# One-head attention pass of a graph network: node-block steps at fixed phases of a slot

## The chip, the cores and the metric

The kernel runs on one core of one Trainium2 chip. The metric is the device time of one execution in microseconds (us). Lower is better.

## What is computed

A graph of 3125 nodes (128 features each) and 103125 edges sorted by destination goes through four residual layers. The third is a pair of GATv2 layers, the fourth a pair of typed transformer layers. Cut to what matters here:

```python
def gatv2(x, src, dst, Wl, bl, Wr, br, att, bias, heads, out_ch):
    xl = (x @ Wl + bl).reshape(n, heads, out_ch)
    xr = (x @ Wr + br).reshape(n, heads, out_ch)
    e = leaky_relu(xl[src] + xr[dst], 0.2)
    score = einsum('ehc,hc->eh', e, att)
    smax = segment_max(score, dst)
    ex = exp(score - smax[dst])
    alpha = ex / (segment_sum(ex, dst)[dst] + 1e-16)
    return segment_sum(xl[src] * alpha, dst) + bias      # plus self loops
...
x = x + gatv2(relu(gatv2(layernorm_relu(x), ..., heads=4)), ..., heads=1)
h = layernorm_relu(x)
k, q, v = (typed_linear(h, node_type, W) for W in (Wk, Wq, Wv))   # 8 node types
kw, m = rel_apply(k, edge_type, Watt), rel_apply(v, edge_type, Wmsg)  # 8 relations
```

The typed layer's key and value are made for all eight relations of a node at once, before its edges are looked at, and are gathered by edge afterwards.

## The kernel before, in words

The nodes lie in 25 blocks of 128 (numbered k, in the order in which their edges are processed). The edges are cut into 830 tiles of 128, none across two blocks, and 16 tiles make a group; there are 52 groups. Six passes go over all groups: one weighted sum, then attention passes 1 to 5. This case is about pass 3, the GAT with one head (H = 1), from about 3325 to 4491 us of the span. Its node-block work is class `AfterGats`: when all edges of a block have been summed, the block's attention is finished, its features are normalized, and the typed key, query and value tables that pass 4 reads are made and written.

In `attention_pass` (L924) each engine runs its own list of slots. Slot s does the first half of group s (gathered rows plus destination rows, leaky relu, scores) and the second half of group r = s - 1 (segment maxima by scans, exponentials, weighted rows, sums). All queues are in order and wait on semaphores.

- POOL (`gather_rows`, L749 to L763) issues 16 indirect DMAs a group (L761), into one of 4 buffers. It waits until group s - 4 has been weighed.
- PE in slot s (L1347 to L1392): destination rows of products 0 (L1293), `turn_scores(r)` (L1308, L1310), own rows 0 (L1302), destination rows 1, hooks 0 and 1, `spread_drop` (L1317), `turn_back` (L1322, L1324), hook 2, destination rows 2, hook 3, sums 0 to 2 (L1341, a unit of up to three tiles each), own rows 2, hook 4, destination rows 3, sums 3, hook 5, sums 4 and 5, hook 6, hook 7.
- DVE in slot s (L1212 to L1271): the rest of the additions of group s - 2 (L1201) around the scans of tiles (L1128, L1129), hooks 0 and 1, the chain over tiles with product 0 in it (L1140 to L1176), score 0 (L1122), `rescale` (L1182), hook 2, last maxima and weighing (L1186, L1189), hook 3, product and score 1 (L1111, L1113, L1122), additions 0, hook 4, additions 1 and 2, hook 5, product and score 2, additions 3, hook 6, product and score 3, hook 7.
- ACT in slot s (L1069 to L1088): `keep_scores` (L1045), hook 0, `keep_column` (L1027), hook 1, `open_scale` (L1049, an exponential), `exps` (L1053), `exp_columns` (L1058), `weigh_tiles` (L1066), hooks 2 to 6, `keep_linear` (L1038), hook 7.
- SP issues the loads of one-hot matrices and flags of the next slot, with hooks 0 to 3 ahead of the flags and 4 to 7 behind them.

A hook is a place where the node-block work stands in an engine's list. Hook number x counts 8 a slot, so x = 8s + h. `first(k)` (L1469) gives the x at which block k begins, and each step of the block has an offset d from it: step d runs at x = first(k) + d. With `last_tile(k)` in group s at place t, `first` is 8(s + 1) + 6 where t < 11 and 8(s + 2) otherwise. So the phase (the hook within a slot) of every step differs between the two kinds of blocks. Blocks 9 to 13, 23 and 24 are of the second kind, the other eighteen of the first. A block is 33.2 tiles, so a new one begins nearly always two slots after the one before (three once, from 13 to 14).

The node-block steps of `AfterGats` (L2163 to L2259), before:

- DVE: d = 0 own shares (L1918 to L1929), d = 3 the new features and their statistics (L1938 to L1941, L2220 to L2222, L1513 to L1515), d = 6 `standard` (L1526, L1527), d = 9 `by_type` (L2094: the turned block times eight type masks).
- ACT: d = 2 exponential (L2235), d = 5 square root (L1520), d = 7 normalized features (L2240) and clearing of the sums (L2242), d = 13 `take_kv`, `take_query` (L2136, L2141), d = 15, 17, 19, 21 `take_relations` 0 to 3 (L2151).
- PE: d = 8 `turn` (L2085), d = 11 `key_and_value` (L2106, 16 products), d = 12 `query` (L2113), d = 14, 16, 18, 20 `relations` 0 to 3 (L2129). `relations` i waits until ACT has taken i - 1 (L2126).
- SP: d = -4 load of the block's masks (L2069), d = 26 write of the block's table (L2160).

An ACT table load stands in ACT's list just ahead of the first instruction that needs another table: one of L1520 (square root) and one of L1049 (exponential) for each block.

Of the kernel before, what the change touches and what calls it, by code (L numbers as in the profile page):

```python
# [14 lines left out]
P = 128  # L15
# [9 lines left out]
J = 4  # L25
GT = GC * J
NT_MAX = (E + NB * (P - 1)) // P
NG = (NT_MAX + GT - 1) // GT
# [15 lines left out]
TYPES = 8  # L44
# [7 lines left out]
HOOKS = 8  # L52
# [26 lines left out]
class Chain:  # L79


    def __init__(self, sem):
        self.sem, self.n = sem, 0
# [1349 lines left out]
def last_tile(k):  # L1433

    return (k + 1) * NT_MAX // NB - 1
# [19 lines left out]
class After:  # L1455


    LAST = 0
    EARLY = 0

# [8 lines left out]
    def first(self, k):  # L1469

        s, t = divmod(last_tile(k), GT)
        return HOOKS * (s + 1) + 6 if t < ON_TIME else HOOKS * (s + 2)

    def due(self, x):

        return [(k, x - self.first(k)) for k in range(NB) if -self.EARLY <= x - self.first(k) <= self.LAST]

    @property
    def end(self):
        return self.first(NB - 1) + self.LAST + 1  # L1480

# [9 lines left out]
    def load(self, sp, s):  # L1491
        pass

    def sp(self, sp, x):
        pass

    def act(self, act, x):
        pass

    def pe(self, pe, x):  # L1500
        pass

    def dve(self, dve, x):
        pass
# [25 lines left out]
class AfterL0(After):  # L1530


    LAST = 13

# [236 lines left out]
class AfterL1(Projected):  # L1771


    LAST = 23

# [132 lines left out]
def own_shares(after, dve, c, k, H, att):  # L1908

    e, V = after.e, after.nc.vector  # L1910
    hs = D // H
    W = hs + 1
    a = e.acc[:, k * AW:k * AW + H * W].rearrange("p (h c) -> p h c", c=W)
    edge_max = e.acc[:, k * AW + H * W:k * AW + H * W + H]
    own, em, top = after.scalars(k, 0, H), after.scalars(k, 4, H), after.scalars(k, 8, H)
    share = after.scalars(k, 32, 2 * H)
    t = after.t
    c.step(dve, V.tensor_tensor(t, e.xlN[:, k, :], e.kN[:, k, :], ALU.add))  # L1918
    if H == 1:
        c.step(dve, V.scalar_tensor_tensor(t, t, 0.0, att, ALU.max, ALU.mult, accum_out=own))  # L1920
    else:
        c.step(dve, V.scalar_tensor_tensor(t, t, 0.0, att, ALU.max, ALU.mult))
        c.step(dve, V.tensor_reduce(own, t.rearrange("p (h c) -> p h c", h=H), AX, ALU.add))
    c.step(dve, V.tensor_tensor(own, own, e.xlW[:, k, D:D + H], ALU.add))
    c.step(dve, V.tensor_scalar(em, a[:, :, hs], 0.5, -BIG, ALU.is_lt, ALU.mult))
    c.step(dve, V.tensor_tensor(em, em, edge_max, ALU.add))
    c.step(dve, V.tensor_tensor(top, em, own, ALU.max))
    V.tensor_tensor(share[:, 0:H], em, top, ALU.subtract)
    return V.tensor_tensor(share[:, H:2 * H], own, top, ALU.subtract)  # L1929


def scaled_shares(after, dve, c, k, H):

    e, V = after.e, after.nc.vector
    W = D // H + 1
    a = e.acc[:, k * AW:k * AW + H * W].rearrange("p (h c) -> p h c", c=W)
    den, share = after.scalars(k, 12, H), after.scalars(k, 32, 2 * H)
    c.step(dve, V.tensor_tensor(den, a[:, :, W - 1], share[:, 0:H], ALU.mult))  # L1938
    c.step(dve, V.tensor_tensor(den, den, share[:, H:2 * H], ALU.add))
    c.step(dve, V.reciprocal(den, den))  # L1940
    return V.tensor_tensor(share.rearrange("p (n h) -> p n h", n=2), share.rearrange("p (n h) -> p n h", n=2),  # L1941
                           den.unsqueeze(1).to_broadcast([P, 2, H]), ALU.mult)


class AfterGat(Projected):


    LAST = 16

# [76 lines left out]
BANDS = 4  # L2026
# [4 lines left out]
class Typed(After):  # L2031


    def __init__(self, nc, A, e, name):
        super().__init__(nc, A, e, name)
        ar = e.arena
        self.kqv, self.bd = ar[:, 0:3072], ar[:, 3072:3584]
        self.stage, self.kvS = ar[:, 3584:5632], ar[:, 5632:5888]
        self.temps = [ar[:, 5888 + P * n:5888 + P * (n + 1)] for n in range(5)]
        self.mask, self.hTm = ar[:, 6528:7040].bitcast(BF16), ar[:, 7040:8064]  # L2040
        self.wa = ar[:, 8064:9088]
        self.left, self.right = e.ps[:, 7, 0:256], e.ps[:, 7, 256:512]
        self.corner = e.ps[:, 7, 384:512]
        self.pri = e.small[:, 320:320 + RELS]

    def load_typed(self, sp, n, name, layer, home, done):
# [32 lines left out]
    def turn(self, pe, src, ready, k, free, frees):  # L2079

        S, nc = self.S, self.nc
        pe.wait_ge(S[ready], k + 1)
        if frees > 0:
            pe.wait_ge(S[free], frees)
        nc.tensor.transpose(self.corner, src, self.e.ident[:, :]).then_inc(S["turned"], 1)  # L2085

    def by_type(self, dve, n, k, free, frees):

        S, V = self.S, self.nc.vector
        dve.wait_ge(S["mask_here"], 16 * (k + 1))  # L2090
        dve.wait_ge(S["turned"], n)
        if frees > 0:
            dve.wait_ge(S[free], frees)
        V.tensor_tensor(self.hTm.rearrange("p (t n) -> p t n", t=TYPES), self.corner.unsqueeze(1).to_broadcast([P, TYPES, P]),  # L2094
                        self.mask.rearrange("p (t n) -> p t n", t=TYPES), ALU.mult).then_inc(S["masked"], 1)

    def key_and_value(self, pe, k, masked):
# [65 lines left out]
class AfterGats(Typed):  # L2163


    LAST = 26
    EARLY = 4

    def __init__(self, nc, A, e):
        super().__init__(nc, A, e, "n4")  # L2170
        self.t = self.temps[0]
        self.att, self.b2 = e.vecs[:, D:2 * D], e.vecs[:, 256:384]

    def load(self, sp, s):

# [14 lines left out]
    def sp(self, sp, x):  # L2190

        for k, d in self.due(x):
            if d == -4:
                self.load_mask(sp, k, 1)
            elif d == 26:
                self.write(sp, k, self.e.t3_d[0])

    def close(self, sp):
# [3 lines left out]
    def dve(self, dve, x):  # L2202

        e, S, nc, V = self.e, self.S, self.nc, self.nc.vector
        c = self.chain
        if x == 0:
            V.memset(self.bd, 0.0).then_inc(S["bd_zero"], 1)
        if x == 44:
            self.scale_relations(dve, c)
        for k, d in self.due(x):  # L2210
            xk = e.xN[:, k, :]
            if d == 0:
                self.summed(dve, k)
                own_shares(self, dve, c, k, 1, self.att).then_inc(S["shares"], 1)
            elif d == 3:
                dve.wait_ge(S["exp_made"], k + 1)
                if k == 0:
                    dve.wait_ge(S["v"], 16)
                c.step(dve, scaled_shares(self, dve, c, k, 1))
                c.step(dve, V.scalar_tensor_tensor(self.t, e.acc[:, k * AW:k * AW + D], self.scalars(k, 32, 1), self.b2, ALU.mult, ALU.add))  # L2220
                c.step(dve, V.scalar_tensor_tensor(self.t, e.xlN[:, k, :], self.scalars(k, 33, 1), self.t, ALU.mult, ALU.add))
                c.step(dve, V.tensor_tensor(xk, xk, self.t, ALU.add))  # L2222
                self.statistics(dve, c, k, xk, "var")
            elif d == 6:
                self.standard(dve, c, k, "std").then_inc(S["scale"], 1)
            elif d == 9:
                self.by_type(dve, k + 1, k, "q_done", k)

    def act(self, act, x):

        e, S, nc = self.e, self.S, self.nc
        for k, d in self.due(x):
            if d == 2:
                act.wait_ge(S["shares"], k + 1)
                nc.scalar.activation(self.scalars(k, 32, 2), self.scalars(k, 32, 2), ACT.Exp).then_inc(S["exp_made"], 1)  # L2235
            elif d == 5:
                self.deviation(act, k, "var", "std")
            elif d == 7:
                act.wait_ge(S["scale"], k + 1)
                nc.scalar.activation(e.hN[:, k, :], e.xN[:, k, :], ACT.Relu, bias=self.scalars(k, 27, 1), scale=self.scalars(k, 29, 1))\  # L2240
                    .then_inc(S["h_made"], 1)
                nc.scalar.activation(e.acc[:, k * AW:(k + 1) * AW], e.acc[:, k * AW:(k + 1) * AW], ACT.Copy, scale=0.0)  # L2242
            elif d == 13:
                self.take_kv(act, k)
                self.take_query(act, k)
            elif d in (15, 17, 19, 21):
                self.take_relations(act, k, (d - 15) // 2)

    def pe(self, pe, x):

        for k, d in self.due(x):
            if d == 8:
                self.turn(pe, self.e.hN[:, k, :], "h_made", k, "rel_taken", BANDS * k)
            elif d == 11:
                self.key_and_value(pe, k, k + 1)
            elif d == 12:
                self.query(pe)
            elif d in (14, 16, 18, 20):
                self.relations(pe, k, (d - 14) // 2)  # L2259


class FromLayer(Typed):
# [87 lines left out]
class AfterTyped(FromLayer):  # L2350


    LAST = 25
    EARLY = 1

# [67 lines left out]
class AfterAll(FromLayer):  # L2423


    LAST = 20
    EARLY = 1

# [102 lines left out]
```

## Time and profile before

| | |
|---|---|
| median of 3 runs | 6829.93 us (6827.04 to 6832.83) |
| profiled execution | 6820.63 us, span 6818.9 us |
| busy share of the span | PE 69%, PE weight load 58%, DVE 73%, ACT 24%, POOL 70% |
| mean granted TensorE clock | 0.767 |

Times in the rows below are us from the start of the span. A line of the timeline gives the start, the busy time, engine, line of the kernel, operation and operands, how many instructions run together (xN), and in brackets the idle time of the engine just before with what ended it. A line of a stretch gives its two ends, its length, the busy time and number of instructions of each engine (of PE, PE weight load, DVE, ACT and POOL where all are shown, of the one engine where one line of the kernel is), the granted TensorE clock as a share of full speed, the DMA share and GB/s.

### The profile page before, as it was taken

How to read it: one execution, taken by the hardware profiler on the slowest of the kernel's cores; microseconds unless marked ns; L12 is line 12 of the kernel's file. 1: busy time of each engine (PE TensorE's matmuls, PEld its weight loads, DVE VectorE, ACT ScalarE, POOL GpSimd, SP SyncE). 2: the span in 40 equal slices, each digit the busy share in tenths (PEclk: the TensorE clock that was granted, in tenths of full speed). 3: DMA queues.
4: the chain of work that ended last, by engine and by line, in shares of the span. 5: the costliest groups of instructions: out<-in, count | busy, mean ns of one | idle time of the engine just before them, and what ended most of it. 6: DMA issues, size and time to landing. Idle time of an engine off the chain costs nothing. (4 is left out here: it accounts for less than half of the span.)

```text
span 6818.9 us, 92826 instructions
## 1 busy us (share of the span) xinstructions
PE 4690.2 (69%) x26423; PEld 3981.3 (58%) x26423; DVE 4946.8 (73%) x14307; ACT 1667.5 (24%) x5320; POOL 4761.5 (70%) x4997
## 2 busy tenths in 40 slices
PE   3555555666666678787688888857777776676665
PEld 2444444555555566666566666646776765565665
DVE  5434433888888688888688778857777775888887
ACT  3333332122222111111133323312222221112121
POOL 5777776777776677777577777547666663777775
PEclk8676676777776788888789889967778776777777
DMA  5444445666665455545455555556666664666665
GB/s 163 167 160 161 160 153 159 214 212 218 208 217 179 143 165 161 169 157 166 131 189 185 171 177 183 168 175 224 215 226 223 213 214 135 219 218 228 217 230 157
DMA packets 407533, 1266.66 MB, mean 186 GB/s; under 512 B 128582, under 2 KB 189766, under 8 KB 320630
## 3 DMA queue, kind: packets, MB, share of 16 engines
q1 hardware_dynamic: 200000, 760.73, 30.6%
q0 software_dynamic: 199760, 495.12, 26.2%
q10 hardware_dynamic: 7270, 4.88, 0.3%
q8 instruction: 221, 3.62, 0.2%
q14 instruction: 282, 2.31, 0.1%
HBM read 1083.37 MB, written 176.98 MB: 185 GB/s over the span
## 5 line engine op out<-in xcount | busy, mean ns | idle before, releaser
L761 POOL DMA_INDIRECT gathered_rows<-table_l,arena x3048 | 2915.2, 956 | 1073.7 <-issue 911.9
L1201 DVE TENSOR_TENSOR acc<-acc,ps 128x136 f32 (+2 forms) x4160 | 1209.0, 291 | 520.3 <-PE ps L1341 360.3
L1293 PEld LDWEIGHTS ps<-dst_side,onehot_t 128*128 128x128 f32 x8320 | 1312.0, 236 | 445.5 <-issue 369.8
L1293 PE MATMUL ps<-dst_side,onehot_t 128*128 x8320 | 1421.0, 326 | 184.9 <-issue 106.4
L761 POOL DMA_INDIRECT gathered_rows<-table_l,src_rel_edges x1116 | 1060.6, 950 | 624.5 <-issue 329.3
L1341 PE MATMUL ps<-weighted_rows,onehot 128*128 128x136 f32 (+2 forms) x8320 | 1281.3, 315 | 13.7 <-DVE acc L1201 10.1
L1341 PEld LDWEIGHTS ps<-weighted_rows,onehot 128*128 128x128 f32 x8320 | 1226.7, 227 | 46.1 <-issue 35.1
L1122 DVE TENSOR_REDUCE scores<-products 128x16 f32<-128x512 f32 (+2 forms) x1040 | 711.4, 684 | 27.1
L907 PE MATMUL ps<-gathered_rows,onehot 128*128 128x128 f32 x1664 | 340.6, 369 | 471.1 <-ACT gathered_rows L833 469.7
L761 POOL DMA_INDIRECT arena<-table_l,src_rel_edges x544 | 516.2, 949 | 189.1 <-issue 161.8
L863 DVE TENSOR_TENSOR acc<-acc,ps 128x128 f32 x832 | 238.4, 286 | 532.9 <-PE ps L907 500.3
L907 PEld LDWEIGHTS ps<-gathered_rows,onehot 128*128 128x128 f32 x1664 | 294.9, 266 | 525.8 <-ACT gathered_rows L833 525.5
L1317 PE MATMUL ps<-open_node_drop,ones 64*128 64x4 f32 (+2 forms) x520 | 129.4, 319 | 511.0 <-DVE open_node_drop L1158 511.0
L1189 DVE TENSOR_TENSOR weighted_rows<-gathered_rows,ps 128x512 f32<-128x512 f32 x732 | 454.2, 679 | 5.6 <-ACT weighted_rows L1058 5.0
L1317 PEld LDWEIGHTS ps<-open_node_drop,ones 64*128 64x128 f32 (+2 forms) x520 | 108.9, 260 | 571.7 <-DVE open_node_drop L1158 569.2
L1302 PE MATMUL ps<-gathered_rows,ident 128*128 128x512 f32 x624 | 398.5, 725 | 32.8 <-DMA gathered_rows<-table_l,arena 32.7
L1117 DVE TENSOR_TENSOR products<-gathered_rows,ps 128x512 f32<-128x512 f32 x420 | 284.8, 678 | 139.4 <-DMA gathered_rows<-table_l,src_rel_edges 71.0
L833 ACT ACTIVATE gathered_rows<-gathered_rows,arena 128x128 f32<-128x128 f32 x832 | 264.9, 391 | 436.3 <-DMA gathered_rows<-table_l,arena 436.2
L761 POOL DMA_INDIRECT arena<-table_l,arena x272 | 258.6, 951 | 82.9 <-issue 81.3
L2129 PE MATMUL ps<-arena 32*128 32x256 f32 x800 | 268.2, 461 | 33.0 <-ACT arena L2151 31.3
L1322 PE MATMUL ps<-ident,exp_scores_t 64*128 64x64 f32 (+2 forms) x260 | 99.5, 383 | 275.9 <-ACT exp_scores_t L1053 275.9
L1115 DVE SCALAR_TENSOR_TENSOR products<-ps,vectors 128x512 f32<-128x512 f32 x312 | 210.9, 676 | 101.0 <-PE ps L1302 99.9
(321 smaller groups left out, 6206.5 us busy)
## 6 DMA issues: line engine op xcount, KB each, us to landing
onehot_t<-onehots_turned SPq DMA_DIRECT2D x260, 1024.0 KB, 5.3
onehot<-onehots SPq DMA_DIRECT2D x260, 1024.0 KB
onehots<-onehot SPq DMA_DIRECT2D x52, 1024.0 KB, 6.8
onehots_turned<-onehot_t SPq DMA_DIRECT2D x52, 1024.0 KB, 4.3
table_l<-arena SPq DMA_DIRECT2D x50, 1024.0 KB
gathered_rows<-table_l,arena POOLq DMA_INDIRECT x3048, 2.5
segment_flags_sb<-segment_flags SPq DMA_DIRECT2D x1300, 8.2 KB
arena<-type_mask_rows SPq DMA_DIRECT2D x75, 256.0 KB
```

Source lines behind the costliest of these rows:

```text
L761: pool.indirect_dma_start(out=home(v, t // GC)[:, t % GC, :], out_offset=None, in_=table, in_offset=bass.IndirectOffsetOnAxis(ap=index[:, ...
L833: ins = nc.scalar.activation(weighed[:, u, t, :], rv[:, u, t, :], ACT.Copy, scale=e.ewE[:, bass.ds(s * GT + t, 1)])
L863: V.tensor_tensor(a, a, ps[:, bank(u, j), g * P:g * P + D], ALU.add).then_inc(e.added.sem, 1)
L907: ins = nc.tensor.matmul(ps[:, bank(u, j), g * P:g * P + D], e.oh[:, u, GC * j + g, :], weighed[:, u, GC * j + g, :], start=True, stop=True)
L1117: ins = V.tensor_tensor(out, home(v, j)[:, :, 0:D], z, ALU.mult)
L1122: V.tensor_reduce(scE[:, GC * j:GC * (j + 1), :], e.prod[:, j % 2, :].rearrange("p (g h d) -> p g h d", g=GC, h=H), AX, ALU.add).then_inc( ...
L1189: V.tensor_tensor(exvH[:, GC * j:GC * (j + 1), :, 0:hs], home(v, j)[:, :, vrow:vrow + D].rearrange("p g (h d) -> p g h d", h=H), bc(exE[:, ...
L1201: V.tensor_tensor(a, a, ps[:, BP + n % 3, at:at + PW], ALU.add).then_inc(e.acc_step.sem, 1)
L1293: ins = nc.tensor.matmul(ps[:, BZ + k, g * P:(g + 1) * P], e.ohT[:, u, t * P:(t + 1) * P], kRows[:, bass.ds(bs[t % 8], D)], start=not by_p ...
L1302: nc.tensor.matmul(ps[:, BZ + j % 2, :].rearrange("p (g d) -> p g d", d=D), e.ident[:, :], home(v, j)[:, :, 0:D], start=False, stop=True). ...
L1341: ins = nc.tensor.matmul(ps[:, BP + n % 3, at:at + PW], e.oh[:, u, t, :], exvT[:, t, :], start=True, stop=True)
L2129: ins = mm(home, self.kvS[lane, m * P:(m + 1) * P], self.bd[lane, m * RELS * BAND:(m + 1) * RELS * BAND], start=True, stop=True)
```

## The change

`AfterGats` gets a `first` of its own: 8(s + 2) for every block. So a block always begins at hook 0 of a slot, here called its slot A, and slot B is the one behind it. With a new block every two slots, each slot A also holds the steps d = 16 to 23 of the block before, and each slot B its steps 24 to 31. All steps get new offsets. The turned block goes to bank 3 of PSUM, where the exponentials lie (columns 256 to 383), not to a corner of bank 7. So `turn` no longer waits for `rel_taken` of the block before; it waits for `masked` of the block before and, in PE's list, for the weighing by DVE of the last group. `key_and_value` now waits for `rel_taken`. In other classes the turned block stays where it was.

```diff
--- before.py
+++ after.py
@@ -2041,6 +2041,7 @@
         self.wa = ar[:, 8064:9088]
         self.left, self.right = e.ps[:, 7, 0:256], e.ps[:, 7, 256:512]
         self.corner = e.ps[:, 7, 384:512]
+        self.face = self.corner
         self.pri = e.small[:, 320:320 + RELS]
 
     def load_typed(self, sp, n, name, layer, home, done):
@@ -2082,7 +2083,7 @@
         pe.wait_ge(S[ready], k + 1)
         if frees > 0:
             pe.wait_ge(S[free], frees)
-        nc.tensor.transpose(self.corner, src, self.e.ident[:, :]).then_inc(S["turned"], 1)
+        nc.tensor.transpose(self.face, src, self.e.ident[:, :]).then_inc(S["turned"], 1)
 
     def by_type(self, dve, n, k, free, frees):
 
@@ -2091,7 +2092,7 @@
         dve.wait_ge(S["turned"], n)
         if frees > 0:
             dve.wait_ge(S[free], frees)
-        V.tensor_tensor(self.hTm.rearrange("p (t n) -> p t n", t=TYPES), self.corner.unsqueeze(1).to_broadcast([P, TYPES, P]),
+        V.tensor_tensor(self.hTm.rearrange("p (t n) -> p t n", t=TYPES), self.face.unsqueeze(1).to_broadcast([P, TYPES, P]),
                         self.mask.rearrange("p (t n) -> p t n", t=TYPES), ALU.mult).then_inc(S["masked"], 1)
 
     def key_and_value(self, pe, k, masked):
@@ -2163,13 +2164,19 @@
 class AfterGats(Typed):
 
 
-    LAST = 26
-    EARLY = 4
+    LAST = 35
+    TAKES = (24, 25, 29, 31)
+    RELATIONS = (24, 25, 28, 30)
 
     def __init__(self, nc, A, e):
         super().__init__(nc, A, e, "n4")
         self.t = self.temps[0]
+        self.face = e.ps[:, 3, 256:384]
         self.att, self.b2 = e.vecs[:, D:2 * D], e.vecs[:, 256:384]
+
+    def first(self, k):
+
+        return HOOKS * (last_tile(k) // GT + 2)
 
     def load(self, sp, s):
 
@@ -2190,9 +2197,9 @@
     def sp(self, sp, x):
 
         for k, d in self.due(x):
-            if d == -4:
+            if d == 1:
                 self.load_mask(sp, k, 1)
-            elif d == 26:
+            elif d == 35:
                 self.write(sp, k, self.e.t3_d[0])
 
     def close(self, sp):
@@ -2209,10 +2216,10 @@
             self.scale_relations(dve, c)
         for k, d in self.due(x):
             xk = e.xN[:, k, :]
-            if d == 0:
+            if d == 2:
                 self.summed(dve, k)
                 own_shares(self, dve, c, k, 1, self.att).then_inc(S["shares"], 1)
-            elif d == 3:
+            elif d == 5:
                 dve.wait_ge(S["exp_made"], k + 1)
                 if k == 0:
                     dve.wait_ge(S["v"], 16)
@@ -2221,42 +2228,45 @@
                 c.step(dve, V.scalar_tensor_tensor(self.t, e.xlN[:, k, :], self.scalars(k, 33, 1), self.t, ALU.mult, ALU.add))
                 c.step(dve, V.tensor_tensor(xk, xk, self.t, ALU.add))
                 self.statistics(dve, c, k, xk, "var")
-            elif d == 6:
+            elif d == 8:
                 self.standard(dve, c, k, "std").then_inc(S["scale"], 1)
-            elif d == 9:
+            elif d == 15:
                 self.by_type(dve, k + 1, k, "q_done", k)
 
     def act(self, act, x):
 
         e, S, nc = self.e, self.S, self.nc
         for k, d in self.due(x):
-            if d == 2:
+            if d == 3:
                 act.wait_ge(S["shares"], k + 1)
                 nc.scalar.activation(self.scalars(k, 32, 2), self.scalars(k, 32, 2), ACT.Exp).then_inc(S["exp_made"], 1)
-            elif d == 5:
+            elif d == 6:
                 self.deviation(act, k, "var", "std")
-            elif d == 7:
+            elif d == 9:
                 act.wait_ge(S["scale"], k + 1)
                 nc.scalar.activation(e.hN[:, k, :], e.xN[:, k, :], ACT.Relu, bias=self.scalars(k, 27, 1), scale=self.scalars(k, 29, 1))\
                     .then_inc(S["h_made"], 1)
                 nc.scalar.activation(e.acc[:, k * AW:(k + 1) * AW], e.acc[:, k * AW:(k + 1) * AW], ACT.Copy, scale=0.0)
-            elif d == 13:
+            elif d == 21:
                 self.take_kv(act, k)
                 self.take_query(act, k)
-            elif d in (15, 17, 19, 21):
-                self.take_relations(act, k, (d - 15) // 2)
+            elif d in self.TAKES:
+                self.take_relations(act, k, self.TAKES.index(d))
 
     def pe(self, pe, x):
 
         for k, d in self.due(x):
-            if d == 8:
-                self.turn(pe, self.e.hN[:, k, :], "h_made", k, "rel_taken", BANDS * k)
-            elif d == 11:
+            if d == 13:
+                self.e.exv_ready.wait(pe, self.a_no, J * min(x // HOOKS, NG))
+                self.turn(pe, self.e.hN[:, k, :], "h_made", k, "masked", k)
+            elif d == 16:
+                if k >= 1:
+                    pe.wait_ge(self.S["rel_taken"], BANDS * k)
                 self.key_and_value(pe, k, k + 1)
-            elif d == 12:
+            elif d == 20:
                 self.query(pe)
-            elif d in (14, 16, 18, 20):
-                self.relations(pe, k, (d - 14) // 2)
+            elif d in self.RELATIONS:
+                self.relations(pe, k, self.RELATIONS.index(d))
 
 
 class FromLayer(Typed):
```

## Rows read from the trace of the kernel before

**Rows 1.** Stretches of pass 3, DVE line L1128 alone: one scan a slot.

```profile
3805.20:4046.20 241.00, 4.12 (x10) 0.81 0.53 167
4067.30:4437.10 369.80, 7.62 (x18) 0.91 0.57 174
```

**Rows 2.** The gathers of pass 3: ns min/median/max, first and last start.

```profile
L761 POOL DMA_INDIRECT gathered_rows<-table_l,arena x830: 938/944/1384, 3324.8 to 4379.4; - x166
```

**Rows 3.** Timeline of a slot of block 11, PE and DVE.

```profile
3912.62 5.74 PE L2106 MATMUL ps<-arena 128*128 128x128 f32 x32
...
3919.07 2.71 DVE L1201 TENSOR_TENSOR acc<-acc,ps 128x130 f32 x8 [5.27 <-PE ps L1341]
```

**Rows 4.** Timeline of slots 36 and 37, DVE.

```profile
4106.16 0.69 DVE L1122 TENSOR_REDUCE scores<-products 128x4 f32<-128x512 f32 x1
...
4114.44 0.19 DVE L1186 TENSOR_TENSOR weighted_rows<-ps,arena 128x16 f32<-128x16 f32 x1 [0.39 <-ACT weighted_rows L1058]
...
4126.56 0.69 DVE L1122 TENSOR_REDUCE scores<-products 128x4 f32<-128x512 f32 x1
...
4129.56 0.10 DVE L1938 TENSOR_TENSOR row_scalars<-acc,row_scalars 128x1 f32<-128x1 f32 x1
...
4131.94 0.15 DVE L1515 TENSOR_SCALAR row_scalars<-row_scalars 128x1 f32<-128x1 f32 x1
...
4135.99 0.19 DVE L1186 TENSOR_TENSOR weighted_rows<-ps,arena 128x16 f32<-128x16 f32 x1
...
4140.75 0.94 DVE L1201 TENSOR_TENSOR acc<-acc,ps 128x130 f32 x3 [1.34 <-PE ps L1341]
...
4147.32 0.69 DVE L1122 TENSOR_REDUCE scores<-products 128x4 f32<-128x512 f32 x1
```

**Rows 5.** Timeline of slots 36 and 37, ACT.

```profile
4130.96 0.66 ACT L2151 ACTIVATE arena<-ps 128x256 f32<-128x256 f32 x2 [2.55 <-PE ps L2129]
...
4138.99 1.28 ACT L1520 ACT_TABLE_LOAD   x1
4140.28 0.20 ACT L1520 ACTIVATE row_scalars<-row_scalars 128x1 f32<-128x1 f32 x1
4141.99 0.50 ACT L2240 ACTIVATE h_nodes<-x_nodes,row_scalars 128x128 f32<-128x128 f32 x1 [1.50 <-DVE row_scalars L1527]
4142.39 0.30 ACT L2242 ACTIVATE acc<-acc 128x136 f32<-128x136 f32 x1
...
4149.09 1.28 ACT L1049 ACT_TABLE_LOAD   x1
4154.54 0.26 ACT L1049 ACTIVATE open_node_scale<-ps,open_node_column 128x1 f32<-128x1 f32 x1 [4.17 <-PE ps L1317]
```

**Rows 6.** Timeline of slots 36 and 37, PE.

```profile
4127.31 0.39 PE L1308 MATMUL ps<-ident,scores 128*16 128x128 f32 x2 [1.52 <-DVE scores L1122]
...
4129.79 1.13 PE L2129 MATMUL ps<-arena 32*128 32x256 f32 x4
4133.69 0.38 PE L1317 MATMUL ps<-open_node_drop,ones 32*128 32x1 f32 x2 [2.77 <-DVE open_node_drop L1158]
...
4137.34 2.08 PE L1293 MATMUL ps<-dst_side,onehot_t 128*128 x8
...
4149.56 1.05 PE L1293 MATMUL ps<-dst_side,onehot_t 128*128 x8
```

**Rows 7.** Stretches of slots 36 and 37: the granted clock.

```profile
4118.00:4135.20 17.20, 11.77 (x70) 8.53 (x68) 15.15 (x54) 3.15 (x12) 12.93 (x15) 1.00 0.55 175
4135.40:4142.00 6.60, 6.60 (x27) 5.76 (x28) 4.83 (x13) 4.68 (x14) 4.76 (x5) 0.50 0.22 53
```

**Rows 8.** Timeline of the pass's end: last score, last block, next pass.

```profile
4435.05 0.69 DVE L1122 TENSOR_REDUCE scores<-products 128x4 f32<-128x512 f32 x1
...
4467.12 6.71 PE L2106 MATMUL ps<-arena 128*128 128x128 f32 x32 [1.37 <-DVE arena L2094]
...
4491.26 0.06 DVE L1273 MEMSET tile_ends_turned<- 128x2 f32 x1 [24.19 <-PEq L1419]
```

## The prediction

> **What bounds the kernel now.** I read the stretches first. Only pass 3 is touched, so the question is what sets its pace. The scan of tiles runs once a slot. In one stretch it takes 369.8 us for 18 slots, 20.5 us each; in the stretch of blocks 9 to 13 it takes 241 us for 10 slots, 24.1 us each [rows 1]. Then the gathers: 830 of them start between 3324.8 and 4379.4 us, 1.27 us apart, 20.3 us a group [rows 2]. The last score of the pass ends at 4435.7 [rows 8], 56 us after the last gather was issued. So the gathers are ahead, and slots, not gathers, set the end: their pace is a floor only.
>
> The timelines say what a slot consists of. In the stretch of blocks 9 to 13 the key and value products stand at hook 3, ahead of sums 0: PE works 5.74 us on them and DVE waits 5.27 us for the sums [rows 3]. That is the cost of that phase. Two blocks' worth: a pair of slots is 48.2 us there (241/5), against 41.2 us in slots 36 and 37, from score end to score end 4106.85, 4127.25, 4148.01, that is 20.4 + 20.8 [rows 4]. Five pairs times 7 us is 35 us lost to the second phase: the most that an equal phase for all could give back, and a little of the lag if the pace came down to the floor.
>
> **The change part by part.** Nothing is added or taken from the work, apart from waits. So I take the pair 36/37 and move its steps, and then look for what is late.
>
> *Slot A* is slot 36 with these moves. Own shares go from hook 6 to hook 2, ahead of the weighing: same length, and they cover the wait of 0.39 us for the exponentials [rows 4]. The new features and statistics (from 4129.56 to 4132.09, 2.5 us [rows 4]) come in at hook 5. The products stay in the head of the slot (hook 0 for hook 1, nothing stands between). The query goes behind the sums, where PE has room. 20.4 + 2.5 - 0.4 = 22.5 us. What is late next: PE. Product 2 starts 2.5 us later, while PE has nothing else to do; by my count PE has idle times of about 1 and 2.6 us just before the head of slot B, with one destination-row batch of 1.05 us between them. The square root waits for the statistics at hook 6; `keep_linear` behind it has until the scores are made, some 4 us later, so nothing waits.
>
> *Slot B* is slot 37 without the 2.5 us of statistics, and without the 1.34 us in which DVE waits for sums [rows 4]: relation 3 of the block before no longer stands between the turning back and the destination rows (it did, until 4137.34 [rows 6]). 20.8 - 2.5 - 1.3 = 17.0 us. `standard` stays in that slot, `by_type` at hook 7 as before.
>
> Without any new wait the pair is 39.5 us. But the head of slot B now carries a queue on ACT. Behind `keep_scores` stand relation 0 taken (hook 0), `keep_column`, then at hook 1 relation 1 taken, the normalized features, the clearing, then the table load for the exponential, because the square root ran last; only then `open_scale` and `exps`, for which DVE and the whole second half of the slot wait. From the last score's end: PE has relation 0 done after 3.7 us (4127.25 to 4130.92 [rows 4, 6]); ACT takes it in 0.66; PE makes relation 1 in 1.13, which waits for that take; ACT takes it in 0.66; features and clearing are 0.8, the load 1.28, `open_scale` 0.26 [rows 5]. With small gaps that is 8.5 us, and DVE starts its last maxima some 0.9 us after it (exponentials, turning back, copy), at 9.4. In slot 37 that came at 8.7 (4135.99 [rows 4]), and 2.5 us of it were the statistics, which go, and 0.3 us is `standard`, which comes: 6.5. So slot B waits 2.9 us anew, and the pair is 42.4 us. Before, the table load ran at 4149.09, and ACT was then idle for 4.17 us, so it cost nothing [rows 5]; it loses that cover.
>
> One rule of the Trainium skill makes this worse: the page "ScalarE: Activation LUTs", section "What ACT_TABLE_LOAD costs", has a drain of about 1.38 us behind each load of 1.28. By it slot B would wait 1.4 us longer, some 30 us over the pass. Here the square root starts at 4140.28, right behind its load of 1.28 us begun at 4138.99 [rows 5]: no drain shows, so the row is used.
>
> *The clock.* After PE's idle time of 2.77 us in the head of slot 37 [rows 6] the granted clock is 0.50 for the 6.6 us that follow, after 1.00 before it [rows 7]: 1.2 instead of 2.4 GHz. A batch of destination rows takes 2.08 us in that stretch and 1.05 outside it [rows 6]. Now the idle time comes just before the head of slot B (1 and 2.6 us), so the head itself would run at the lower level, and it is the head that ACT's queue hangs on. All of the 3.7 us up to relation 0 at half speed would cost 3.6 us more, none 0. I take 2.3, nearer to the whole, since the stretch at the lower level lasted 6.6 us, but it may begin a little after the head does. A second drop behind the longer wait for ACT (about 3 us of idle PE) lies where slot 37 has its own; DVE has 3 us of its own work before it needs sums there. I take 0.5 us for it, between 0 and 3. The pair is then 45.2 us.
>
> *Smaller things.* The mask load moves from d = -4 to d = 1. On SP it stands behind `by_type` of the block before, ahead of the flags, which are due a slot later; its data have 14 hooks. The write at d = 35 has five hooks until the stage is filled again, as before. `turn` in bank 3 waits for a weighing for which sums 3 just ahead of it has already waited: nothing. POOL waits more often, being ahead: nothing.
>
> *The end of the pass.* From the last score to the next pass it is 55.5 us now, of which 24.1 follow the start of the last block's products at 4467.12 [rows 8]. The last block's own shares come some 2 us earlier. But the products, query and relations of block 23, formerly partly inside slots 51 and 52, now run after slot 52, and in ACT's list the square root and the features of block 24 stand behind takes of block 23. I count 29.6 us at full clock and 38 at half until the last products, against 31.4 now: between -2 and +7, I take +4 us.
>
> **The sum.** Seventeen pairs of the first kind (all eighteen but block 0's, which has no relations before it and stays about equal): 17 x (45.2 - 41.2) = +68. Five pairs of the second kind: 5 x (45.2 - 48.2) = -15. End: +4. Together +57 us with 45.2; I shade the pair to 44.9, as the two clock terms hardly come whole in every pair: 17 x 3.7 - 5 x 3.3 + 4 = +50 us. On the profiled execution's 6820.6 us that is 6871. The median of the runs is 9.3 us above that execution, so 6880 us.
>
> **Rivals.**
> 1. *Faster: ACT's queue doesn't bind.* If relations and takes in the head go through beside DVE's work, the pair falls to 39.5 us, under the gathers' floor of 40.6, which then sets the pace: 17 x (-0.6) + 5 x (-7.6) + 4 = -44 us, 6786. For it: ACT is busy only 24% and its wait at 4154.54 is 4.17 us of spare time [rows 5]. Against: the list is in order, and the sum of rows gives 8.5 us where 5.6 are free. It decides at 5.6 us from the last score to `open_scale`.
> 2. *The queue binds, the clock holds.* Pair 42.4: 17 x 1.2 - 5 x 5.8 + 4 = -5 us, 6825. For it: after 1.52 us of idle PE at 4127.31 [rows 6] the clock was still 1.00 [rows 7]. Against: the idle time is longer now.
> 3. *The clock stays low through all of slot B.* Then the pair is as in the second kind, 48.2: 17 x 7 + 4 = +123 us, 6953. For it: PE's busy share of a pair falls with its length. Against: that kind also had the products ahead of the sums.
>
> **How the numbers follow.** The forecast (44.9 us a pair, or anything from 43 to 47) has 0.53, rival 1 0.22, rival 2 0.17, rival 3 0.08. 0.2%, about what a measurement of this kernel can tell, is 13.7 us. Rival 2 straddles it: I give 0.12 of it to no change and 0.05 to faster. The forecast at its lowest, 43, is +9 us (17 x 1.8 - 5 x 5.2 + 4), so 0.03 of it is no change too. Faster 0.27, same 0.15, slower 0.58. The range goes from 6800, which takes in rival 2 with its spread and stops short of rival 1 whole, to 6930, the forecast at 47 us a pair (+97).
>
> **What would show it.** In the changed profile: the scan of tiles at 22 to 23 us a slot over the whole pass, with no stretch at 24.1 and none at 20.5; in slots B `open_scale` 8 to 12 us after the last score, with the table load right ahead of it and DVE idle at `rescale` by 2 to 5 us, released by ACT; the wait of 5.27 us for sums gone; the granted clock at 0.5 in the head of slots B; gathers waiting for the weighing in most slots. The prediction is wrong if `rescale` in slots B waits less than 1 us, or if the pace comes out at 20.3 us a slot. Passes other than the third should stay within a microsecond or two.

## The result, and the profile after

The changed kernel takes 6878.56 us (median of 4 runs, 6871.19 to 6884.97), the kernel before 6828.49: a ratio of 1.0077, 95% interval 1.0064 to 1.009, so 50 us slower. Forecast were 6880 us. All of it lies in pass 3. In the profiled executions it goes from first gather to next pass's first from 1167.1 to 1228.5 us, +61 us; the last score of the pass comes at 4488.1 instead of 4435.7 [rows 8], and the rest is the end and a start that differs by 5 us. The profiled execution itself took 6876.83 us, 56 more than that of before.

The stretches of the changed kernel, DVE line L1128 alone (one scan a slot; columns as in [rows 1]), from the scan of group 8 to that of group 50, and parts of it. The three parts hold 12, 10 and 14 slots; in the last two the scans at both ends are counted:

```profile
3522.00:4467.80 945.80, 17.18 (x42) 0.83 0.53 170
...
3522.10:3802.00 279.90, 4.90 (x12) 0.81 0.53 175
3847.40:4066.60 219.20, 4.10 (x11) 0.85 0.53 174
4152.60:4467.90 315.30, 5.72 (x15) 0.84 0.52 165
```

There are 42 slots in 945.8 us, 22.5 each or 45.0 us a pair; the three parts have 23.3, 21.9 and 22.5 us a slot, so none is at 20.5 and none at 24.1. The same 42 slots took 895.3 us before, at a clock of 0.88:

```profile
3518.40:4413.70 895.30, 17.75 (x42) 0.88 0.58 181
```

What DVE waited for in pass 3, changed kernel (us in total, times, longest):

```profile
DVE acc L1182 <- ACT open_node_scale L1049: 105.2, 46, 5.5
DVE acc L1201 <- PE ps L1341: 46.5, 80, 1.5
DVE tile_ends_turned L1273 <- PEq L1419: 25.9, 1, 25.9
DVE products L1115 <- PE ps L1302: 25.7, 14, 11.5
DVE weighted_rows L1186 <- ACT weighted_rows L1058: 13.2, 23, 0.6
```

and the same view of the kernel before:

```profile
DVE acc L1201 <- PE ps L1341: 65.4, 55, 5.3
DVE tile_ends_turned L1273 <- PEq L1419: 24.2, 1, 24.2
DVE products L1115 <- PE ps L1302: 21.7, 7, 12.1
...
DVE acc L1182 <- issue: 8.5, 35, 0.8
...
DVE acc L1182 <- ACT open_node_scale L1049: 4.9, 17, 0.6
```

The wait of 5.27 us for sums [rows 3] is gone: the longest is now 1.5 us. In its place `rescale` (L1182) waits 105 us for ACT, where it waited 4.9 before: 88.7 us of it in slots B, 16.1 in slots A. How, the head of one slot B shows (timelines of ACT, then PE, then DVE, changed kernel; lines behind 2041 are one higher or more than before):

```profile
4173.71 0.27 ACT L1045 ACTIVATE scores_t<-ps 16x128 f32<-16x128 f32 x1 [4.53 <-PE ps L1310]
4178.52 0.66 ACT L2152 ACTIVATE arena<-ps 128x256 f32<-128x256 f32 x2 [4.55 <-PE ps L2130]
4179.07 0.20 ACT L1027 ACTIVATE open_node_column<-onehot_t 128x1 f32<-128x1 f32 x1
4181.34 0.66 ACT L2152 ACTIVATE arena<-ps 128x256 f32<-128x256 f32 x2 [2.07 <-PE ps L2130]
4181.89 0.49 ACT L2247 ACTIVATE h_nodes<-x_nodes,row_scalars 128x128 f32<-128x128 f32 x1
4182.27 0.31 ACT L2249 ACTIVATE acc<-acc 128x136 f32<-128x136 f32 x1
4182.59 1.28 ACT L1049 ACT_TABLE_LOAD   x1
4183.88 0.26 ACT L1049 ACTIVATE open_node_scale<-ps,open_node_column 128x1 f32<-128x1 f32 x1
```

```profile
4173.06 0.39 PE L1308 MATMUL ps<-ident,scores 128*16 128x128 f32 x2 [2.40 <-DVE scores L1122]
...
4174.57 1.86 PE L1293 MATMUL ps<-dst_side,onehot_t 128*128 x8
4176.36 2.07 PE L2130 MATMUL ps<-arena 32*128 32x256 f32 x4
...
4184.39 0.28 PE L1322 MATMUL ps<-ident,exp_scores_t 16*128 16x16 f32 x1 [3.08 <-ACT exp_scores_t L1053]
```

```profile
4172.32 0.69 DVE L1122 TENSOR_REDUCE scores<-products 128x4 f32<-128x512 f32 x1
...
4184.18 0.30 DVE L1182 TENSOR_TENSOR acc<-acc,open_node_scale 128x129 f32 x1 [4.97 <-ACT open_node_scale L1049]
```

The last score ends at 4173.01, `open_scale` at 4184.14: 11.1 us later, in the order forecast, take, column, take, features, clearing, load. DVE is idle for 4.97 us. PE was idle 2.40 us ahead of the head, then its clock fell within it: the destination rows take 1.86 us and relation 0 2.07 us, not 1.13 [rows 6].

Not every slot B is like this one. In another, the clock held (PE, ACT and DVE, and the stretch, all engines, of the changed kernel):

```profile
4311.15 0.39 PE L1308 MATMUL ps<-ident,scores 128*16 128x128 f32 x2 [1.45 <-DVE scores L1122]
...
4319.27 0.26 ACT L1049 ACTIVATE open_node_scale<-ps,open_node_column 128x1 f32<-128x1 f32 x1
...
4319.56 0.30 DVE L1182 TENSOR_TENSOR acc<-acc,open_node_scale 128x129 f32 x1 [2.54 <-ACT open_node_scale L1049]
```

```profile
4311.10:4317.10 6.00, 4.74 (x24) 2.99 (x24) 5.53 (x21) 1.38 (x6) 4.48 (x6) 1.00 0.73 263
```

Here `open_scale` ends 8.4 us behind the last score (4311.09), and DVE waits 2.54 us. Of the 21 slots B with relations in their head (the last slot left out), five are so: PE was idle 1.2 to 1.6 us ahead of the head, and the granted clock of the six microseconds behind the score is 1.00. In the other sixteen PE was idle 2.40 us there, that clock is 0.55 to 0.72, `open_scale` ends 10.1 to 11.4 us behind the score, and DVE waits 3.8 to 5.5 us.

### The profile page after: what moved, and what is told of

It reads as the page before. It is cut to its first block and busy times, and to the rows that moved or that the text cites. A ratio compares the mean times of both kernels' runs of the same rounds, so it can differ in the third digit from the quotient of the medians.

```text
span 6875.1 us, 92851 instructions
## 1 busy us (share of the span) xinstructions
PE 4757.0 (69%) x26423; PEld 4031.3 (59%) x26423; DVE 4947.1 (72%) x14307; ACT 1666.6 (24%) x5320; POOL 4760.8 (69%) x4997
## 5 line engine op out<-in xcount | busy, mean ns | idle before, releaser
L1341 PE MATMUL ps<-weighted_rows,onehot 128*128 128x136 f32 (+2 forms) x8320 | 1313.1, 320 | 20.4 <-issue 12.5
L1341 PEld LDWEIGHTS ps<-weighted_rows,onehot 128*128 128x128 f32 x8320 | 1254.3, 231 | 56.2 <-issue 46.5
```

The lines of the kernel that those rows point to most:

```text
L1341: ins = nc.tensor.matmul(ps[:, BP + n % 3, at:at + PW], e.oh[:, u, t, :], exvT[:, t, :], start=True, stop=True)
```

## The experiments

Ten kernels ran. "Slot B" and offsets are as in the section on the change. The runs of before beside them had medians of 6826 to 6828 us. Runs 1 to 4 were made together on one chip. The changed kernel was not among them: its first four runs (6878.56 us) are of another time, and on that same chip it took 6894.35 us later (run 9). So a difference of some 15 us between runs 1 to 4 and the changed kernel can't be told. The scan pace is given for the 42 slots between the scans of groups 8 and 50.

**1. Relations behind.**

```diff
-    TAKES = (24, 25, 29, 31)
-    RELATIONS = (24, 25, 28, 30)
+    TAKES = (28, 29, 30, 31)
+    RELATIONS = (28, 29, 30, 31)
```

> The changed kernel with the four relation products and their takes moved out of the head of slot B, to hooks 4, 5, 6 and 7 (d = 28 to 31 on PE and ACT). ACT's queue as the cause: only features, clearing and the table load stand ahead of open_scale, which comes at about 5 us from the last score instead of 10.9; the wait of rescale in slots B falls from about 5 us to under 1, a pair from 45 us to 41, the whole by 80 to 95 us, to 6785 to 6800 us, below the kernel before. The low clock in the head as the main cause: the head is as slow as now, the wait falls by 1 us at most, 6855 us. Product 2 coming late in slot A as the cause: no change, 6878 us.

Measured: 6893.61 us (6887.91 to 6898.87), ratio 1.0097 (1.008 to 1.0114): 15 us above the first runs of the changed kernel and level with those on the same chip, so no gain, where 80 to 95 us were expected of the queue theory. The wait at `rescale` in slots B did fall to 0.2 us, as the queue theory said (38.1 us in the pass are left, nearly all in slots A), but a new one of 81.4 us stands at the scan of tiles (DVE's waits, this kernel):

```profile
DVE tile_scans L1128 <- ACT scores_t L1045: 81.4, 50, 3.7
DVE acc L1201 <- PE ps L1341: 43.9, 67, 2.8
DVE acc L1182 <- ACT open_node_scale L1049: 38.1, 24, 2.3
```

and its PE timeline says why:

```profile
4192.38 1.12 PE L2130 MATMUL ps<-arena 32*128 32x256 f32 x4
4194.25 1.12 PE L2130 MATMUL ps<-arena 32*128 32x256 f32 x4 [0.75 <-ACT arena L2152]
4195.40 2.05 PE L1293 MATMUL ps<-dst_side,onehot_t 128*128 x8
4197.38 0.61 PE L1308 MATMUL ps<-ident,scores 128*16 128x128 f32 x2
```

The score that L1308 turns was there at 4193.04, but relations 2 and 3, with the take between them, and the destination rows at the lower clock stood ahead of it in PE's list until 4197.4. I had emptied the head of slot B and filled its end. The end costs as much: from last score to last score slot B takes 18.7 us instead of 23.0, but slot A, whose scan waits for that end, 26.6 instead of 22.4. The queue moved, and the wait moved with it. So this run confirms what waits, but my sum for it was wrong, as it looked at one end of the slot only.

**2. Features behind, and 3. root behind** take parts of ACT's queue out of the head without touching the relations.

```diff
-            elif d == 9:
+            elif d == 10:
                 act.wait_ge(S["scale"], k + 1)
```

> The changed kernel with only the normalized features and the clearing moved behind the exponentials on ACT (d = 9 to d = 10, hook 1 to hook 2 of slot B): 0.8 us less ahead of open_scale. ACT's queue as the cause: 0.8 us a slot B, 18 us in all, 6861 us, with the wait of rescale about 4.2 us. Any other cause: no change, 6878 us.

```diff
-            elif d == 6:
+            elif d == 11:
                 self.deviation(act, k, "var", "std")
...
-            elif d == 9:
+            elif d == 13:
                 act.wait_ge(S["scale"], k + 1)
```

(and on DVE `standard` at 12, on PE `turn` at 14.)

> The changed kernel with the square root moved from slot A to slot B behind the exponentials (d = 6 to 11, standard 8 to 12, features 9 to 13, turn 13 to 14): features, clearing and the table load, 2.1 us, leave the head of slot B; the two takes stay. ACT's queue as the cause: open_scale at about 8.8 us instead of 10.9, 2.1 us less a slot B, 46 us in all, 6832 us. If the load is hidden anyway: only the 0.8 us of features, 6861 us. If the clock is the cause: no change, 6878 us.

Measured: features 6868.09 us (6864.13 to 6872.10), root 6849.09 (6845.32 to 6851.62). Against the changed kernel's 6878.56 that is 10 and 29 us, against its 6894.35 on the same chip 26 and 45, where 18 and 46 were expected. DVE's wait at `rescale` over the pass: 105.2 us in the changed kernel, 86.1 with the features behind, 66.5 with the root behind. These are 19.1 and 38.7 us less for 22 full slots B, 0.87 and 1.76 us each, against 0.8 and 2.1 us of work taken out. The clock of the heads differs between the profiles, so slots B are better compared at the same clock. With 0.72 granted over the six microseconds behind the last score, `open_scale` in the changed kernel, with the features behind and with the root behind:

```profile
4228.48 0.26 ACT L1049 ACTIVATE open_node_scale<-ps,open_node_column 128x1 f32<-128x1 f32 x1
```

```profile
3623.07 0.26 ACT L1049 ACTIVATE open_node_scale<-ps,open_node_column 128x1 f32<-128x1 f32 x1
```

```profile
3617.27 0.27 ACT L1049 ACTIVATE open_node_scale<-ps,open_node_column 128x1 f32<-128x1 f32 x1
```

The scores before them ended at 4218.68, 3613.84 and 3609.47: 10.1, 9.5 and 8.1 us. So each piece of the queue counts in full, the table load among them (the last difference is 1.4 us, its own time 1.28).

**4. PE kept busy.** A method called behind the destination rows 0 of slot B:

```diff
+        if any(d == 8 for k, d in self.due(x)):
+            self.e.exv_ready.wait(pe, self.a_no, J * (x // HOOKS - 1))
+            for n in range(8):
+                self.nc.tensor.matmul(self.e.ps[:, 3, 384:512], self.e.ident[:, :], self.e.ident[:, :], start=True, stop=True)
```

> The changed kernel with 8 extra products of the identity on PE (about 2.1 us at full clock) in slot B, ahead of the turning of scores, where PE is idle 2.4 us now; nothing reads them. The clock term as predicted, 2.3 us a slot B: the head runs at clock 1.0, relation 0 is done 3.7 us after the last score instead of 5.4, the wait of rescale falls by 1.7 to 2.3 us, the whole by 35 to 50 us, to 6830 to 6845 us. If the clock costs nothing (ACT's queue alone): no change or up to 0.3 us a slot more, 6878 to 6885 us.

Measured: 6864.19 us (6852.60 to 6866.64), 14 us less than the first runs of the changed kernel and 30 less than those on the same chip, where 35 to 50 were expected: more work made it faster, but by less than expected. In 17 of the 21 slots B `open_scale` now ends 8.4 to 8.5 us behind the score, what the rows had given for the full clock (8.5). One of the other four, at 9.0 us, where the clock dips (ACT's timeline and two stretches, all engines, of this kernel):

```profile
4163.29 1.28 ACT L1049 ACT_TABLE_LOAD   x1
4164.58 0.26 ACT L1049 ACTIVATE open_node_scale<-ps,open_node_column 128x1 f32<-128x1 f32 x1
```

```profile
4155.90:4161.90 6.00, 5.17 (x24) 3.15 (x24) 5.43 (x21) 1.02 (x4) 4.48 (x6) 0.91 0.63 231
4166.20:4171.20 5.00, 5.00 (x24) 5.00 (x25) 4.10 (x10) 2.00 (x7) 3.50 (x4) 0.52 0.15 32
```

The score before it ended at 4155.87, so `open_scale` ends 9.0 us later here; relation 0 is done at 4159.53, 3.7 us behind the score. The wait at `rescale` is 71.5 us instead of 105.2, 33.7 less or 1.5 a slot B, where 1.7 to 2.3 were expected of the clock term. But the drop came later instead: the five microseconds behind the wait for ACT run at a granted clock of 0.52, and the waits of additions for sums grew from 46.5 to 58.1 us. That led to the last experiment.

**5. Relations spread.** Relation 0 at the end of slot A, where PE is idle, one relation in the head of slot B with its take behind the exponentials, two behind as before.

```diff
-    TAKES = (24, 25, 29, 31)
-    RELATIONS = (24, 25, 28, 30)
+    TAKES = (23, 26, 29, 31)
+    RELATIONS = (23, 24, 28, 30)
```

> The changed kernel with relation 0 moved to the end of slot A (PE and ACT d = 23, where PE is idle) and only relation 1 left at hook 0 of slot B, its take behind the exponentials (d = 26). Nothing is packed at the end of slot B, as it was in the run with all four relations behind. ACT's queue as the cause: open_scale in slots B about 5.5 us after the last score, the wait of rescale under 1 us in all slots, a pair at 41 us or less, the whole 6785 to 6805 us. If PE or the products at hook 0 bind the pair anyway: 43 to 44 us a pair, 6850 us.

Measured: 6784.58 us (6780.93 to 6787.50), ratio to before 0.9939 (0.9923 to 0.9956). Four numbers of the change make 94 us against its first runs, which is more than the change lost. The stretch and DVE's waits of this kernel:

```profile
3521.90:4377.00 855.10, 17.23 (x42) 0.89 0.57 187
```

```profile
DVE acc L1201 <- PE ps L1341: 43.0, 67, 1.5
...
DVE acc L1182 <- ACT open_node_scale L1049: 17.3, 24, 1.8
```

A pair takes 40.7 us, and the wait of 105 us is down to 17, nearly all of it in slots A. The gathers alone take 40.6, but between 3600 and 4300 us no engine waits for gathered rows here, nor in runs 6 and 7. So these runs come out at the pace of the gathers; that the gathers hold them there is not shown.

**6. The same with the root behind**, edits of 3 and 5 together.

> The same, and the square root with what follows moved behind the exponentials of slot B (d = 11, 12, 13, turn 14), so that the table load too leaves the head. ACT's queue as the cause: a further 0 to 0.5 us a pair, since the head was already short enough; 6780 to 6800 us, at the floor of the gathers of 40.6 us a pair. If the load still counts: 1.3 us a pair below the run without it.

Measured: 6785.34 us (6781.49 to 6790.42), 40.7 us a pair: no difference from 5. Once the takes are gone, the load fits in the head: in run 5 `open_scale` ends 4.9 us behind the score (4157.20 against 4152.30), before DVE asks for it. So the load as such costs nothing; it does so only at the end of a queue that is too long.

**7. Before, one phase.** The kernel before with nothing changed but `first` of `AfterGats`:

```diff
+        return HOOKS * (s + 1) + 6 if t < ON_TIME else HOOKS * (s + 2) + 6
```

> The kernel before, with all its offsets, and only first changed: blocks of the second kind begin at hook 6 of the later slot, so that every block has the phases of the first kind. The 48.2 us pairs as the cost of the second phase alone: they become 41 us, 35 us less, 6795 us, and up to 5 us more for an end that begins later. If something else made slots 22 to 31 slow: no change, 6828 us.

Measured: 6780.33 us (6774.07 to 6783.74), ratio 0.9934 (0.9917 to 0.9951): 46 us less than before. The second phase was the whole cost of slots 22 to 31: those five pairs fall from 242.8 to 205.0 us, 38 less, where 35 were expected. The last score of the pass comes at 4388.6 instead of 4435.7, 47 us earlier: besides the 38, the last pair, where block 23 ran at the second phase too, gives 4, and 3 come from an earlier start of the pass. Behind the last score the end is 5 us longer, so the pass as a whole is 39.5 us shorter in the profiles. It is the fastest kernel here with those of runs 5 and 6, and all three beat the two given ones; the 4 or 5 us between them are within their scatter. Its stretch:

```profile
3515.30:4371.00 855.70, 17.53 (x42) 0.89 0.59 188
```

**8. Before, face moved.** Only the turned block in bank 3, with `masked` and a weighing as what `turn` waits for, `key_and_value` waiting for `rel_taken`:

```diff
+        self.face = e.ps[:, 3, 256:384]
...
-                self.turn(pe, self.e.hN[:, k, :], "h_made", k, "rel_taken", BANDS * k)
+                self.e.exv_ready.wait(pe, self.a_no, J * (min(x // HOOKS, NG) - (x % HOOKS < 4 and x // HOOKS <= NG)))
+                self.turn(pe, self.e.hN[:, k, :], "h_made", k, "masked", k)
             elif d == 11:
+                if k >= 1:
+                    pe.wait_ge(self.S["rel_taken"], BANDS * k)
```

> The kernel before with only the turned block in the bank of exponentials: turn waits for masked of the block before and for a weighing that is one slot back where it stands ahead of the sums, key and value products wait for rel_taken. The bank as harmless: no change, 6828 us within 5. If the shared bank costs waits of its own: some us a pair slower, 6840 us or more.

Measured: 6824.46 us (6818.08 to 6827.13), ratio 0.9997 (0.9987 to 1.0006). The bank costs nothing and gains nothing.

**9. The changed kernel again, and 10. PE kept busy twice**, on one chip, with 10 more products behind `spread_drop` of slot B (`after.fill(pe, x, 10)`).

> The changed kernel itself, on the chip of the next run, so that the two can be compared: 6878 us.

> The changed kernel with 8 extra products ahead of the turning of scores in slot B, as in the run before, and 10 more (2.6 us at full clock) behind the spreading of the drop, where PE waits 3 us for the exponentials; nothing reads them. Second drop of the clock as a cost: with the first filling alone DVE waited 58 us for sums in the pass instead of 47; with both filled the clock holds from the head into the sums, that wait falls by 10 to 20 us, and the whole is 25 to 40 us below the changed kernel, 6840 to 6853 us. The second drop as costless: as with one filling, 6864 us.

Measured: changed kernel 6894.35 us (6882.04 to 6915.46), filled twice 6834.47 (6827.34 to 6844.62), ratio of the latter to before 1.0011 (1.0002 to 1.002). The latter is 60 us below the changed kernel on the same chip and 44 below its first runs, more than the 25 to 40 expected. DVE's waits in the pass, filled twice:

```profile
DVE acc L1182 <- ACT open_node_scale L1049: 72.3, 46, 3.5
DVE tile_ends_turned L1273 <- PEq L1421: 28.8, 2, 25.5
DVE weighted_rows L1186 <- ACT weighted_rows L1058: 26.8, 25, 2.6
DVE products L1115 <- PE ps L1302: 20.7, 6, 12.0
DVE acc L1201 <- PE ps L1341: 14.6, 32, 1.5
```

```profile
3520.60:4423.60 903.00, 17.22 (x42) 0.93 0.56 178
```

The waits for sums fell from 58.1 to 14.6 us, the granted clock of the stretch is 0.93 instead of 0.83, and a pair takes 43.0 us instead of 45.0. What is left at `rescale`, 72.3 us, is ACT's queue near full clock: 57.7 us in slots B, 14.4 in slots A. The extra products probably cost something themselves (the 26.8 us at L1186, 13.2 in the changed kernel), so 43.0 is an upper bound for a pair with the queue alone.

## Why the prediction was right, point by point

- **The bound.** Right: slots, not gathers, set the pace. Runs 5 and 7 come down to 40.7 us a pair against the 40.6 of the gathers, and even there nothing waits for gathered rows.
- **ACT's queue, 2.9 us a slot B.** Right in mechanism and near in size. Runs 2 and 3 move the wait piece by piece, run 5 removes it, and run 4 at full clock has relation 0 done 3.7 us behind the score, as summed. The wait at `rescale` in run 4, near full clock, is 57.1 us over 22 slots B, 2.6 us each; 14.1 us more stand in slots A, which the forecast did not have.
- **The table load loses its cover.** Right; at 1.28 us without a drain behind it, as the rows had it: in the head above `open_scale` starts 1.29 us after the load does, and at the same clock the load took 1.4 us of the head with it (runs 2 and 3). What the page "ScalarE: Activation LUTs" of the Trainium skill gives for the drain, 1.38 us, shows in none of these runs.
- **The clock.** Right in mechanism, mis-sized in both terms. The first (2.3 us a slot B) measured 33.7 us less waiting in run 4, 1.5 us each: five of 21 heads kept the full clock, and in thirteen of the other sixteen it fell only after the head had begun. The second (0.5, between 0 and 3) was too low: filling it too (run 10 against run 4) took 922.9 to 903.0 us for 21 pairs, 0.95 us each. The stretch of run 4 is this line:

```profile
3523.20:4446.10 922.90, 17.18 (x42) 0.88 0.54 174
```

  In total the two terms came to 2.0 us a pair in the first profile (run 10's 43.0 against 45.0), where I had 2.8 (2.5 after the shading). In the profile of run 9 the changed kernel was slower still, 46.1 us a pair.
- **The pair.** 44.9 to 45.2 forecast, 45.0 measured; the queue alone 42.4 forecast, 43.0 or less in run 10. But it is a sum of errors that cancel. From last score to last score, over the 20 pairs that begin in slots 8 to 30 and 35 to 49, slot A takes 22.4 us, as forecast (22.5). Slot B takes 23.0 us in the changed kernel, 21.9 in run 4, 20.7 in run 10 and 18.5 in run 5. So its parts are about 18.5 us without the queue (forecast 17.0), 2.2 for the queue (2.9), 1.1 for the first drop (2.3) and 1.2 for the second (0.5). Most of what the base lacks is the 1.34 us of DVE waiting for sums that I took off: in run 5 it still waits 33 us for them in the 24 slots B, 1.4 each.
- **The count of pairs.** One of the seventeen isn't of the kind: block 14 comes three slots after block 13, so its slot B has no relations in its head, and `rescale` waits 0.2 us there. The 20 others take 45.4 us each.
- **The five pairs of the second kind.** The forecast had 35 us lost there; undoing them took 38 off these pairs (run 7). That term was a little small.
- **The end of the pass.** +4 us forecast; from last score to next pass's first gather 56.1 and 60.2 us, so +4.1.
- **The signs.** In slots B `open_scale` ends 8.4 to 11.4 us behind the score (8 to 12 said) and DVE waits 2.5 to 5.5 us (2 to 5 said). The clock of 0.5 in the head shows in sixteen slots of 21 only in part (0.55 to 0.72 over six microseconds) and in five not at all. The passes ahead end 5 us earlier, more than the microsecond or two that I allowed.
- **The bank, the masks, the write.** Nothing, as forecast (run 8 for the bank; the others weren't tried alone).
- **The rivals.** The first, that the queue doesn't bind, falls with runs 2, 3 and 5. The second, queue without clock, falls with run 10: filled twice the kernel takes 6834 us, close to the 6825 of that rival, and the changed kernel takes 44 to 60 more. The third, a pair at 48.2, didn't come, but run 9 had 47.3 us a pair in its last third.

The direction and the mechanism were foreseen; that the number came within 2 us is luck. The base of slot B was 1.5 us too low, the queue and the first drop 0.7 and 1.2 too high, the second drop 0.7 too low. And the eight runs of the changed kernel reach from 6871 to 6915 us, so one of them could have been 35 us off the forecast.

## What to carry to other kernels

Where in-order queues of several engines serve one chain, a step costs by what waits behind it, and nothing by its length where nothing does: four offsets made 94 us (run 5 against the changed kernel's first runs), with the same instructions. Sum up the queue ahead of the one instruction that the others wait for, on each engine and at both ends of the slot, since emptying the head by filling the end gained nothing (run 1). And look for what is moved out of an idle time: a table load that was free, and matrix products that had kept the clock up.

## What the runs showed of the hardware that was not expected

- Extra matrix products whose results nobody reads made a kernel 44 to 60 us faster, with a granted clock of 0.93 instead of 0.83 over 42 slots of the pass. Filling only the first of two idle times gave 14 to 30 us of it: the waits for sums behind the second grew from 46.5 to 58.1 us.
- 2.40 us of idle PE ahead of the head of slot B went with a lower clock in the head in sixteen slots of one execution; 1.2 to 1.6 us left it at 1.00 in five.
- The changed kernel scatters more than any other here: 6871 to 6915 us, against 6817 to 6837 for the kernel before. Its pairs were 46.7, 43.8 and 45.0 us in three stretches of one execution, with the same work in each. Part of it is the clock: in the profile of run 9 no head of a slot B took 8.4 us, as five had in the first profile, and `rescale` waited 118.0 us instead of 105.2. But of the 39 us between these two executions only 23 lie in pass 3; 13 lie ahead of it, and for those no cause is known.
